# Attention slots of a fused attention and mixture-of-experts layer: the turn of the decayed keys, the scores and the state update in a row, and the router's products in another order

## What is computed

```python
# attention branch: 16 heads of 32, chunks of 128 tokens, state S carried over the chunks
q, k, v = silu(xn @ Wq), silu(xn @ Wk), silu(xn @ Wv)
scores  = einsum(q, k) * D            # decay mask, per head and chunk
o_intra = einsum(scores, v)
o_inter = einsum(q, S) * q_decay
S_new   = chunk_decay * S + einsum(k * k_decay, v)
gate    = (xn @ Wg1) @ Wg2            # o * sigmoid(gate), normed per head, then @ Wo
# experts branch: 8 experts, top 2, capacity 1280 slots
probs   = softmax(xn @ Wg)            # router
pos     = cumsum(one_hot(chosen)) - 1 # a token's place in its expert's queue
out     = relu(x[slots] @ w1) @ w2    # scattered back with the gate values
```

## Time and profile before

| | us |
|---|---|
| median of 3 runs | 2031.12 |
| the profiled execution | 2029.56 |
| its span in the trace | 2027.8 |
| PE busy (matmuls, 11048) | 2003.6 |
| DVE busy | 899.4 |
| POOL busy | 723.9 |
| ACT busy | 550.3 |

### The profile page before, as it was taken

How to read it: one execution, slowest core, us unless ns; L and a number is a source line. 1 busy time by engine, 2 the same in 40 slices (tenths; PEclk the granted TensorE clock), 3 DMA queues, 4 the chain that set the end, 5 groups by cost and what they waited for, 6 DMA issues and landing times.

```text
span 2027.8 us, 27700 instructions
## 1 busy us (share of the span) xinstructions
PE 2003.6 (99%) x11048; PEld 1656.6 (82%) x11048; DVE 899.4 (44%) x1792; ACT 550.3 (27%) x986; POOL 723.9 (36%) x600
## 2 busy tenths in 40 slices
PE   7999999999999999999999999999999999999998
PEld 6888888888888888888888888888888888888886
DVE  7777777767752234324333422522342224324311
ACT  6322232223242123123212312411242123123211
POOL 4555544454442224323332431432142214233211
PEclk9999999999999999999999999999999999999999
DMA  7012121202342124214233421521162125224121
GB/s 243 24 64 85 33 74 64 85 28 80 125 148 33 43 58 146 42 59 115 65 67 74 128 45 52 133 62 31 47 155 44 35 47 159 38 63 103 38 32 21
DMA packets 85501, 151.37 MB, mean 75 GB/s; under 512 B 18304, under 2 KB 18304, under 8 KB 85360
## 3 DMA queue, kind: packets, MB, share of 16 engines
q1 hardware_dynamic: 61312, 105.64, 16.2%
q0 software_dynamic: 24048, 43.76, 12.4%
HBM read 109.82 MB, written 39.53 MB: 74 GB/s over the span
## 4 chain that ended last, share of the span: by engine, by line
PE 97%; ACT 1%; issue 1%; DVE 0%; POOL 0%; DMA 0%; POOLq 0%; ACTq 0%
PE bank L1232 49%; PE bank L1496 34%; PE bank L1360 4%; PE bank L1239 2%; PE bank L1551 2%; PE bank L1286 2%; PE bank L1349 1%; PE bank L1327 1%; PE bank L1343 1%; PE bank L1260 1%; PE bank L1320 0%; PE bank L1371 0%; ACT intra_decay L679 0%; DMA out_rows<-x_res 0%; DMA ld_row<-in_L_attn_log_decay 0%
## 5 line engine op out<-in xcount | busy, mean ns | idle before, releaser
L1179 DVE SCALAR_TENSOR_TENSOR h_lo<-bank,h_hi 128x512 fp32r<-128x512 f32 x254 | 175.4, 691 | 749.7 <-ACT h_hi L826 749.4
L618 POOL DMA_INDIRECT gathered<-xn_rows,gather_row x304 | 319.7, 1052 | 478.7 <-DVE x_blocks L1045 294.0
L1232 PE MATMUL bank<-xT_hi,w_hi 128*128 128x512 f32 x1024 | 399.4, 390 | 0.7 <-issue 0.6
L1232 PE MATMUL bank<-xT_hi,w_lo 128*128 128x512 f32 x1024 | 398.7, 389 | 0.0
L1232 PE MATMUL bank<-xT_lo,w_hi 128*128 128x512 f32 x1024 | 398.7, 389 | 0.0
L1496 PE MATMUL bank<-w_hi,h_hi 128*128 128x512 f32 x1016 | 395.7, 389 | 0.3 <-DVE h_lo L1179 0.3
L1496 PE MATMUL bank<-w_hi,h_lo 128*128 128x512 f32 x1016 | 395.8, 390 | 0.0
L1496 PE MATMUL bank<-w_lo,h_hi 128*128 128x512 f32 x1016 | 395.7, 389 | 0.0
L826 ACT ACTIVATE h_hi<-bank 128x512 fp32r<-128x512 f32 x254 | 151.8, 598 | 802.3 <-PE bank L1232 802.2
L631 POOL DMA_INDIRECT out_rows<-y,add_row x80 | 128.9, 1611 | 544.9 <-ACT y L819 473.1
L1232 PEld LDWEIGHTS bank<-xT_hi,w_hi 128*128 128x128 f32 x1024 | 192.2, 188 | 42.3 <-issue 2.5
(11 more groups left out here) (203 smaller groups left out, 2339.3 us busy)
## 6 DMA issues: line engine op xcount, KB each, us to landing
raw_weights<-in_L_ffn_w SPq DMA_DIRECT2D x256, 256.0 KB, 11.5
x_in<-in_L_attn_x SPq DMA_DIRECT2D x32, 256.0 KB, 3.3
xn_rows<-xn SPq DMA_DIRECT2D x32, 256.0 KB, 2.5
x_res<-in_L_attn_x SPq DMA_DIRECT2D x32, 256.0 KB, 4.4
out_rows<-y_attn SPq DMA_DIRECT2D x28, 256.0 KB, 2.0
gathered<-xn_rows,gather_row POOLq DMA_INDIRECT x304
out_rows<-y,add_row POOLq DMA_INDIRECT x80, 5.1
attn_raw<-in_L_attn_Wq SPq DMA_DIRECT2D x4, 256.0 KB, 4.9
```

The lines of the kernel that those rows point to most:

```text
L618: pool.indirect_dma_start(xg[:, nth % 2, q * P:(q + 1) * P], None, xn_pieces, bass.IndirectOffsetOnAxis(ap=gather_row[:, col, q:q + 1], ax ...
L1179: v_.scalar_tensor_tensor(lo[:, 0:n * P], h_bank[f % 2][:, 0:n * P], 0.0, hi[:, 0:n * P].bitcast(F32), ALU.max, ALU.subtract).then_inc(S[" ...
L1232: last = mm(dest, at(left[l], t), at_r(right[r], t), start=(i == 0), stop=(i == n - 1))
```

## The change

In slots with `i > 0` the turn of the decayed keys stands first, then the scores, then the update, and only then gate, next q and next k. In slots with `i == 0` the order stays. At a super's end `project_small` stands ahead of `attend`, `turn_logits` directly behind `attend` and ahead of all four `project_v`, and `count` behind them, next to the following `score`. The turned logits go to bank 7 in place of bank 6, so that they need not wait until the attention output has been read; `turn_kd` in exchange waits until they are read. ScalarE copies the logits before the gate's parts, and VectorE makes the gate's low parts ahead of `gate_output`.

```diff
             def gate_high(g):
                 act.wait_ge(S["small_projected"], g + 1)
+                a.copy(logitsT[LOG_BOTH, :], proj[0][LOG_BOTH, :]).then_inc(S["logits_copied"], 1)
                 a.copy(g1T_parts[0:HD, :], proj[0][0:HD, :])
                 a.copy(g1T_parts[HD:2 * HD, :], proj[0][0:HD, :]).then_inc(S["g1_hi_made"], 1)
-                a.copy(logitsT[LOG_BOTH, :], proj[0][LOG_BOTH, :]).then_inc(S["logits_copied"], 1)
...
             def read_logits(g):
                 dve.wait_ge(S["logits_turned"], g + 1)
-                both = o_bank[:, LOGITS].rearrange("p (t part e) -> p t e part", part=2, e=EXPERTS)
+                both = t_bank[:, LOGITS].rearrange("p (t part e) -> p t e part", part=2, e=EXPERTS)
...
+                if i == GROUPS - 1 and g < SUPERS - 1:
+                    gate_low(g + 1)
                 gate_output(u)
...
                 if i == GROUPS - 1 and g < SUPERS - 1:
-                    gate_low(g + 1)
                     read_logits(g + 1)
...
             def turn_logits(g):
                 pe.wait_ge(S["logits_copied"], g + 1)
-                wait(pe, ("gated_ready", GROUPS * g))
+                wait(pe, ("states_ready", GROUPS * g))
...
             def turn_kd(u):
                 pe.wait_ge(S["kdT_ready"], u + 1)
                 wait(pe, ("states_ready", u))
+                pe.wait_ge(S["logits_read"], u // GROUPS + 1)
...
             for u in range(ATTN_UNITS - 1):
                 g, i = u // GROUPS, u % GROUPS
+                if i > 0:
+                    turn_kd(u)
                 score(u)
-                turn_kd(u)
-                if i == 0:
+                if i > 0:
+                    update_states(u)
+                else:
+                    turn_kd(u)
...
                 project("q", u + 1, proj[0], "q_projected")
-                update_states(u)
+                if i == 0:
+                    update_states(u)
                 pe.wait_ge(S["tanh_ready"], u + 1)
                 project("k", u + 1, proj[1], "k_projected")
+                if i == GROUPS - 1:
+                    pe.wait_ge(S["q_ready"], u + 2)
+                    project_small()
...
                 if i == GROUPS - 1:
-                    pe.wait_ge(S["q_ready"], u + 2)
-                    project_small()
+                    turn_logits(g + 1)
                     pe.wait_ge(S["k_ready"], u + 2)
                     project_v(TPG * (g + 1))
                     pe.wait_ge(S["g1_lo_made"], g + 2)
-                    turn_logits(g + 1)
                     project_v(TPG * (g + 1) + 1)
                     pe.wait_ge(S["v_ready"], TPG * (g + 1) + 1)
                     project_v(TPG * (g + 1) + 2)
-                    count(g + 1)
                     pe.wait_ge(S["v_ready"], TPG * (g + 1) + 2)
                     project_v(TPG * (g + 1) + 3)
+                    count(g + 1)
```

More of the change, by code:

```diff
@@ L1291, in turn_logits @@
                 pe.wait_ge(S["logits_copied"], g + 1)
-                wait(pe, ("gated_ready", GROUPS * g))
+                wait(pe, ("states_ready", GROUPS * g))
                 for j in range(TPG):
                     first = LOGITS.start + j * 2 * EXPERTS
-                    last = nc.tensor.transpose(o_bank[:, first:first + 2 * EXPERTS], logitsT[LOG_BOTH, j * P:(j + 1) * P],
+                    last = nc.tensor.transpose(t_bank[:, first:first + 2 * EXPERTS], logitsT[LOG_BOTH, j * P:(j + 1) * P],
                                                ident[LOG_BOTH, LOG_BOTH])
```

## The result

The changed kernel takes 2035.05 us (median of 19 runs, 2033.57 to 2035.94), the kernel before, in as many runs beside it, 2030.44: +4.6 us, a ratio of 1.0022 with a 95% interval of 1.0015 to 1.0028. Forecast were +5.0 us on 2031.12. The profiled execution of the changed kernel is one of its slower ones (2035.58, span 2033.8), that of the kernel before one of its faster ones, so its steps have to be read one by one and not as a difference of spans.

The account below looks back on a forecast made before the run. PE bounds the kernel, busy 2003.6 of 2027.8 us. Terms 3.7 + 0.05 + 2.3 - 2.2 + 0.6 + 0.55 = +5.0 on 2031.12 gave 2036.1 us; 8-in-10 range 2032.8 to 2039.6, sum's low end about +1.7, high about +9.

Parts of the forecast that it names:

- A: Slots with i > 0: the update, now behind the scores' row tiles, pays one more return; +0.16 in 23 slots, +3.7 us.
- D: Count behind the last v: masks start 1.06 us later, PE waits about 0.2 in supers 1, 3 and 5; +0.6 us.
- B: The turn, now right behind the attend, waits for kdT: 0.45 us in 4 slots, 0.5 more in slot 2; +2.3 us.
- C: Super's end, 7 times: small product 1.81 instead of 2.00, the four v uninterrupted; -0.31 each, -2.2 us.
- E: Program start: ScalarE copies logits first, so PE's first logits' turn waits for the gate's low parts; +0.55 us.
- free returns: First rival: the return costs nothing where the update follows the scores; sum +0.4, time 2031.5 us; chance 0.14.
- the third: Rival: the return from float32 to float32r costs, each merging saves one, 0.13 in a slot; 2027.0 us; chance 0.05.
- The second: Rival: VectorE late at each super's start, even ones too, and the return costs 0.25; 2039.7 us; chance 0.15.
- theory S: From the experiments: each change between full array, row tiles and column tiles costs, wherever it comes; +0.16 in 16 slots.

Follow-up runs that it names:

- the first three experiments: Each against the kernel before: the slots' order alone, 2035.79 us; only the turn ahead of the scores, 2035.68 us; scores in two halves around the turn, 2042.84 us.

## Why the prediction was right

**The verdict and its size** hold: +5.0 forecast, +4.6 measured, and the kernel is slower (the interval starts at 1.0015, below the 0.2% line that the prediction drew, but clear of 1). The terms do not all hold by themselves, and part of the closeness is luck: A is 0.9 too high, D 0.2, and slot 29 (0.25) and the last slot (0.1) bring some of it back. The low end of the sum, +1.7, can't be worked out again from the terms: their own low ends give +0.5, and A's low end with D at nothing gives +3.2, so that the range starts lower than its reason says.

**A (turn, scores, update)**: the pieces came out as written, 0.59, 1.10, 1.09 and 5.48. Two things in the step were wrong. The charge was put on the update's move, and the turn-alone kernel refutes that: with the update left in place the slots cost the same. And with the wrong owner of the price I counted 23 slots. The order has one more change of tile mode only where the turn stands behind an attend (column tiles, full array, row tiles, full array, where it was column tiles, row tiles, full array). Behind the output projection there was a full array already, and the number of changes stays the same; these seven slots cost 0.02 to 0.06 each. "The turn stands behind a tiled product either way" failed there. That is -0.9 us of the 3.7.

**B (waits for kdT)**: right in place and size. Five waits in the profile; slot 1 and the three other even supers cost 0.60 to 0.61 with A's share in it, slot 2 0.58. The odd ones have no wait: with the slots' order alone they are at +0.18, 0.02 above A's share. What the changed kernel has there beyond it (+0.22 to +0.25 in slots 5, 13 and 21) belongs to D. The last odd one, slot 29, has another owner: ScalarE's copy of kd was late by 0.2, which the cover of 0.4 read in slot 11 did not show. There ScalarE splits weights of the experts ahead of it (2.18 us), and with the update left in its old place (the turn alone) the slot is at +0.18.

**C (a super's end)**: -0.28 to -0.34 where nothing else disturbs, forecast -0.31. Only 0.17 of it, the small product's, is a change of tile mode less; that is what is left with the count at its old place. The other 0.12 is the last v, which took 2.83 behind the count where 12 x 0.227 = 2.72.

**D (the later count)**: VectorE's delay was right (1.0 at the masks, 0.74 at the last state, forecast 1.06 and 0.80), PE's wait was smaller: 0.07 ahead of the attend and 0.06 inside it, 0.13 instead of 0.2. The second part shows in the chain at slot 12, before and now:

```profile
233.35 0.89 PE bank L1343 x8
236.54 1.02 PE bank L1345 x8
```

That part falls behind the attend's start and so into the next slot's step; it is what the slots 5, 13 and 21 have above A's share. It goes when the count or the normalisings give way (0.00 in both kernels), and stays with the slots in the old order (+0.08).

**E (the start)**: 0.62, forecast 0.55.

Of the rivals, free returns are refuted by the first three experiments, and so is the third, by which each slot would have got 0.13 shorter: none did. The second, VectorE late in even supers, did not come: the last state there still ends 0.23 ahead of the attend.

The rule of the Trainium skill, TensorEngine Tiling (Array Packing), Key Properties, that a change of the tiling mode drains the engine, is what theory S says in other words. The trace agrees, at 0.19 us for a change here, and the pair that no row of before showed, a full float32 turn followed by row tiles, is no exception: the scores enter at 1.10.

## What to carry to other kernels

Where TensorE is the bound, count the changes between full, row-tiled and column-tiled products in one turn of the loop, before and after, at each place the loop body has a different neighbour; a reorder that puts alike data types together can still add one. Then ask of every product that moves forward what it stood behind: here 1.1 us of scores hid GpSimd's part, and five of 24 turns ran into it. A merge that delays a product by microseconds has to be checked on the engine that reads its result, as the output projection ahead of the attend shows.

## What was not expected of the hardware

An entry into row tiles costs as much as a return to the full array, 0.2 us each, even if the products on both sides are float32 and only 16 matmuls long (two halves of 0.66 against 1.10). And the 19 runs of one and the same kernel that stood beside the changed one, the kernel before, spread over 2 us (2029.26 to 2031.34). Only one of them was profiled, but the profiles of all eleven kernels show two places where such a spread can come from. At the start 0, 7, 12 or 14 of the distances between q's and k's matmuls are above 0.4 us instead of 0.23 (7 in the kernel before, 0 with the slots' order alone, though the two start alike), and the first small product begins between 21.57 and 23.82 us. And what follows the last attend is 0.5 us shorter to 1.3 us longer than in the kernel before. A change of 1.5 us in 2030 is read more surely from the steps of the trace than from the medians.
